# Graph attention in 13 parts from a ring of gathered rows

## The chip, the cores and the metric

The kernel runs on one core of a Trainium2 chip. The metric is the device time of one execution in microseconds (us). Engines are named as the profile names them: PE is the matrix engine, PEld its weight load, DVE the vector engine, ACT the scalar engine, POOL the GpSimd engine, SP the engine that here only issues transfers.

## The reference

The graph has 3125 nodes with 256 features each and 53125 edges, sorted by their destination. Four layers follow each other, each added to its input and normalized: a two-layer mean aggregation, three hops of weighted aggregation, an interaction layer with degree scaling, and graph attention with 8 heads of 32. The change is about the attention:

```python
src = jnp.concatenate([edge_index[0], loop])
dst = jnp.concatenate([edge_index[1], loop])
h = (x @ W).reshape(n, HEADS, OUT_DIM)
a_src = jnp.einsum('nhc,hc->nh', h, att_src)
a_dst = jnp.einsum('nhc,hc->nh', h, att_dst)
e = jax.nn.leaky_relu(a_src[src] + a_dst[dst], NEG_SLOPE)
m = jax.ops.segment_max(e, dst, num_segments=n)
e = jnp.exp(e - m[dst])
denom = jax.ops.segment_sum(e, dst, num_segments=n)
alpha = e / (denom[dst] + 1e-16)
out = jax.ops.segment_sum(h[src] * alpha[:, :, None], dst, num_segments=n)
```

Each node also has an edge to itself (the loop).

## The kernel before, in words

The edges are padded to 416 tiles of 128, the nodes to 25 tiles of 128. Each engine has its own instruction queue, written out in program order; engines wait for each other through semaphores.

The three hops (`hops_pe`, `hop_dve`, `hops_pool`) are six phases of matrix products on PE. DVE empties PSUM banks at the end of each phase (L1552) and applies the activation (L1585, L1590); between phases it prepares small tables for the attention and is otherwise idle. The layer after the hops ends with the projection `h` and the scores of each node; `write_heads` stores them tile by tile to the table `t_h`, whose row is 264 words: 8 heads of 32 values and one word that is 1.0 (`ATT_ROW`, `HEAD_ROW`).

The attention then goes through all edges twice.

1. The score stage. The score of each edge's source node is picked by one-hot products: in 112 steps DVE builds a one-hot of the low part of the index (L2298), PE multiplies the score table with it (L2226), DVE masks by the high part (L2311), and PE sums (L2237). The scores lie with 16 times 8 rows on the partitions and edges along the free dimension, so that a segment maximum is a forward and a backward scan (L2352, L2393, the latter over 3327 elements). Then come the joins between the 16 rows of edges (L2399 to L2409), the subtraction (L2412), transposes (L2415, L2419) and the exponentials on ACT (L2417). Meanwhile POOL gathers rows of `t_h` for part of the edge tiles with indirect DMAs, 128 rows each (L2134); since the final places are still in use as scratch, SP stores those rows to a DRAM table (`keep_rows`) and loads them back later (`load_rows`).

2. The merge. For each quad (4 edge tiles) DVE multiplies the gathered rows with their weights in place (`scale_rows`, L2486) and builds the one-hot of destination nodes (`node_hots`, L2492). Weights of even quads are read from SBUF (`hidden`), those of odd quads from PSUM (`banks`). PE adds each tile's product to a PSUM bank of its node tile (`merge_pe`, L2531): 440 steps, since a tile on a border between node tiles is multiplied twice. The places hold 16 quads; POOL gathers directly into those that are not staged. Early in the merge POOL also gathers the maximum of each node's last edge (`gather_last`, L2453, 25 times) and makes the exponents of the loops (`weigh_own`, L2458). ACT empties the node banks and adds the loop terms.

After the merge DVE divides, normalizes and adds, in seven groups of node tiles (`attended`, `inner_stats`, `inner_norm`, `store`).

## Time and profile before

| | us |
|---|---|
| median of 3 runs | 2983.28 (2981.79 to 2991.97) |
| span of the profiled execution | 2974.2 |
| hops, first to last eviction by DVE | 1122 to 1917 |
| first gather of the attention | 2186.5 |
| first scaling of the merge | 2564.0 |
| first instruction after the merge on DVE | 2900.1 |

The span is the time from the first to the last instruction of the one execution that was profiled; its own device time is not recorded beside it. The median of the runs is 9.1 us above the span, for what lies before the first instruction and behind the last. A busy time says how long an engine executed instructions; the idle time before an instruction is named with what ended it.

### The profile page before, as it was taken

To read this page: it belongs to the slowest core of one execution; us is meant where nothing else is said; L and a number is where in the kernel's file an instruction comes from. 1 tells how busy PE (TensorE), PEld (TensorE's weight loads), DVE (VectorE), ACT (ScalarE), POOL (GpSimd) and SP (SyncE) were. 2 spreads that over 40 slices of the span, in tenths; PEclk is the share of its full clock that TensorE was granted. 3 is DMA by queue.
4 is the path that set the end of the run, shared out by engine and by line. 5 is a ranking of instruction groups with operands and counts; after the bars stand their busy time and mean duration, and the time that the engine had idled before them with its cause. 6 is when DMAs were issued, how large, how long until landed. Compare 5 with 4: busy or idle time off the path is not lost. (4 is left out here: it accounts for less than half of the span.)

```text
span 2974.2 us, 32381 instructions
## 1 busy us (share of the span) xinstructions
PE 2470.6 (83%) x9483; PEld 1621.2 (55%) x9484; DVE 1396.0 (47%) x3940; ACT 707.2 (24%) x1552; POOL 936.7 (31%) x927
## 2 busy tenths in 40 slices
PE   3677789897987999999999999999977886457680
PEld 2444788343766555565556555577743444345560
DVE  7999656455665001030101001455575664546668
ACT  3776545111443000010001000255400000103112
POOL 0000256666666000000000000012167666576740
PEclk9888999998998999999999999999988998678885
DMA  6565678343344743444444434333558887646641
GB/s 233 243 253 225 212 238 264 118 138 97 112 121 137 152 151 129 151 134 151 129 152 133 151 119 145 93 106 102 113 168 271 278 282 245 209 132 190 192 127 43
DMA packets 209534, 493.89 MB, mean 166 GB/s; under 512 B 46457, under 2 KB 128430, under 8 KB 209134
## 3 DMA queue, kind: packets, MB, share of 16 engines
q1 hardware_dynamic: 135185, 301.30, 32.2%
q10 hardware_dynamic: 38173, 133.27, 12.8%
q0 software_dynamic: 36032, 57.60, 7.1%
q8 instruction: 67, 1.10, 0.1%
q14 instruction: 77, 0.63, 0.1%
HBM read 374.71 MB, written 117.32 MB: 165 GB/s over the span
## 5 line engine op out<-in xcount | busy, mean ns | idle before, releaser
L794 POOL DMA_INDIRECT table_dense_weights<-pair_weight,dst x416 | 411.2, 988 | 563.5 <-DVE weights_c L849 324.8
L1526 PE MATMUL banks<-own_term,features_and_rows 128*128 128x391 f32 (+1 forms) x1656 | 552.3, 491 | 0.0
L2134 POOL DMA_INDIRECT features_and_rows<-table_heads,src x376 | 401.7, 1068 | 191.4 <-issue 107.9
L1526 PEld LDWEIGHTS banks<-own_term,features_and_rows 128*128 128x128 f32 x1656 | 312.2, 189 | 226.8
L1552 DVE TENSOR_SCALAR features_and_rows<-banks,hop_bias 128x391 f32<-128x391 f32 (+1 forms) x24 | 15.0, 625 | 762.2 <-PE banks L1526 762.2
L954 PE MATMUL banks<-split_rows,count_columns 128*128 128x512 f32 x1200 | 322.1, 415 | 19.6 <-issue 12.6
L2531 PE MATMUL banks<-features_and_rows,edge_to_window 128*128 x880 | 233.4, 427 | 104.5 <-DVE edge_to_window L2492 71.6
L1526 PE MATMUL banks<-features_and_rows 128*128 128x391 f32 (+1 forms) x840 | 282.4, 491 | 0.0
L954 PEld LDWEIGHTS banks<-split_rows,count_columns 128*128 128x128 f32 x1200 | 226.3, 193 | 76.8 <-issue 21.7
L2531 PEld LDWEIGHTS banks<-features_and_rows,edge_to_window 128*128 128x128 f32 x880 | 181.3, 210 | 156.5 <-issue 122.5
L558 PE MATMUL banks<-features_and_rows,pair_and_bias_rows 128*128 128x400 f16 x806 | 184.3, 388 | 87.1 <-DVE features_and_rows L540 51.9
L936 ACT CAST count_columns<-hidden 128x640 fp32r<-128x640 f16 x310 | 212.4, 723 | 157.2 <-PE banks L954 62.2
L1526 PEld LDWEIGHTS banks<-features_and_rows 128*128 128x128 f32 x840 | 158.4, 189 | 114.6
L2004 POOL DMA_INDIRECT ble_values_at_first_edge<-dst,row_of_first_edge x50 | 48.0, 961 | 516.9 <-DVE ln_rstd L1983 464.9
L1601 POOL DMA_INDIRECT features_and_rows<-table_hop,node_of_tail_row x6 | 5.7, 953 | 638.1 <-DMA table_hop<-tmp 637.1
L558 PEld LDWEIGHTS banks<-features_and_rows,pair_and_bias_rows 128*128 128x128 f16 x806 | 110.8, 152 | 160.9 <-issue 147.6
L540 DVE TENSOR_SCALAR features_and_rows<-counter_fp,features_and_rows 128x400 f16<-128x400 f16 x806 | 198.4, 335 | 0.0
L2226 PE MATMUL banks<-features_and_rows,pair_weight 128*104 128x512 bf16 (+1 forms) x672 | 169.8, 393 | 29.9 <-DVE features_and_rows L2298 19.1
L1543 ACT ACTIVATE features_and_rows<-banks,hop_bias 128x391 f32<-128x391 f32 (+1 forms) x24 | 14.1, 587 | 728.1 <-PE banks L1526 728.1
L1080 PE MATMUL banks<-split_rows,count_columns 128*128 128x258 f32 (+1 forms) x1200 | 158.6, 291 | 13.4 <-issue 10.2
L2237 PE MATMUL banks<-edge_to_window,edge_weight 104*128 104x512 f32 (+1 forms) x224 | 123.1, 634 | 53.2 <-DVE edge_to_window L2311 32.1
L2226 PEld LDWEIGHTS banks<-features_and_rows,pair_weight 128*104 128x104 bf16 x672 | 89.8, 137 | 131.9 <-issue 75.4
(425 smaller groups left out, 3016.8 us busy)
## 6 DMA issues: line engine op xcount, KB each, us to landing
hidden<-table_counts SPq DMA_DIRECT2D x305, 160.0 KB
table_dense_weights<-weights_c ACTq DMA_DIRECT2D x26, 1600.0 KB, 5.7
own_term<-table_dense_weights SPq DMA_DIRECT2D x52, 782.0 KB
features_and_rows<-table_rows_by_edge SPq DMA_DIRECT2D x58, 528.0 KB
own_term<-table_dense_weights SPq DMA_DIRECT2D x34, 780.5 KB
pair_and_bias_rows<-table_edge_rows ACTq DMA_DIRECT2D x50, 512.0 KB
weights_c<-table_edge_rows ACTq DMA_DIRECT2D x50, 512.0 KB
table_rows_by_edge<-features_and_rows SPq DMA_DIRECT2D x48, 528.0 KB
```

The costliest lines, as they stand in the source:

```text
L540: made = e.tensor_scalar(hot_ring[:, s % HOTS, q, :], counter[:, 0:WIDE], steps_key[:, q, s:s + 1], None, ALU.is_equal)
L558: m = e.matmul(banks[:, bass.ds(bank_at, WIDE)], low_ring[:, s // LOWS_AT_ONCE % LOW_BLOCKS, :, 2 * (s % LOWS_AT_ONCE) + q], hot_ring[:, s ...
L794: e.indirect_dma_start(out=self.table, out_offset=bass.IndirectOffsetOnAxis(ap=self.place[:, t:t + 1], axis=0), in_=self.values[:, t:t + 1 ...
L936: e.copy(in_group(count_columns, g), in_group(slot_of(q), g)).then_inc(s_a_wide, 1)
L954: m = e.matmul(to[:, 0:2 * DIM], lhs_of(k), both_pieces(k), start=(k == first), stop=False, skip_group_check=True)
L1080: m = e.matmul(to(wide), count_columns[:, k, :], piece(k, h, wide), start=(k == 0 and h == 0), stop=False, skip_group_check=True)
L1526: m = e.matmul(psum[b][:, 0:wide], z_block(block)[:, f * P:(f + 1) * P], streamed[tile % STREAM][:, lo - from_column:lo - from_column + wi ...
L2004: e.indirect_dma_start(out=t_start[c], out_offset=bass.IndirectOffsetOnAxis(ap=start_at[:, j:j + 1], axis=0), in_=node_pair[:, j, c * HEAD ...
L2134: e.indirect_dma_start(out=to[:, k, :], out_offset=None, in_=t_h, in_offset=bass.IndirectOffsetOnAxis(ap=src[:, t:t + 1], axis=0)).then_in ...
L2226: m = e.matmul(psum[i % 2][head_rows, 0:n], table[:, q, c, :], low_hot[i % 2][c][:, 0:n], start=(c == 0 and q == 0), stop=(c == 1 and q == ...
L2237: e.matmul(psum[2 + b % 2][:, 0:n], sum_heads[head_rows, at:at + P], masked[i % 2][head_rows, 0:n], start=(r == 0), stop=(r == SCAN_ROWS - ...
L2531: e.matmul(banks[:, bass.ds(column_at, ATT_ROW)], onehot[:, k % UNROLL, :], wide_rows[:, bass.ds(row_at, ATT_ROW)], start=False, stop=Fals ...
```

## The change

The attention goes through the edges once, in 13 parts of 32 tiles (8 quads). `t_h` holds the source's score in the 33rd word of each head, so the gathered row itself brings it, and the 112 one-hot steps, the table of edge indices, and the DRAM table of staged rows go away. POOL gathers all 416 tiles in order into a ring of 80 tiles; a quad's place is free once the quad 20 before it has been merged. The condition is written as a count of merge steps: tiles of quad q may be gathered when 4q - 52 steps are done.

For each part, `weigh(b)` takes the scores out of the ring, turns them with PE (256 elements on the free dimension now), runs the scans, joins and exponentials, the exponential now as a polynomial on DVE, and writes weights to PSUM. `prepare(b + 1)` does what does not need the gathered rows of the next part; it stands between the fourth and the fifth quad of part b on DVE. All weights are read from PSUM. Each ring row has 8 words more, with which the merge also sums the exponents of the loops; `gather_last` and `weigh_own` are gone. Loop terms are added by POOL behind its last gather (`add_own`); its rows are loaded from `t_h` by SP after merge step 376 (node tiles 0 to 15) and 385 (the others).

Since a segment can cross a border between parts, the maximum at the 12 borders is found beforehand: for each border POOL gathers 128 rows of 3200 16-bit counts (819 KB) and DVE masks and reduces them (`near_fetch`, `near_counts`), six borders after the first hop's work and six after the second's, with 12 times 4 small operations of 800 elements and fewer at the end. POOL's gathers for the hops stand between them. The rows of destinations, 13 pieces of 1 KB per partition, are loaded in 16 transfers before the last two tiles of `write_heads`. The scatter of start values is one indirect DMA per node tile instead of two. Waits on a register's value are written with one more register operation. `keep_heads` has one copy of 8 elements more.

The core of the diff (indented less than in the file):

```diff
+RING_TILES = 80
+RING_AHEAD = 16
+RING_QUADS = RING_TILES // GROUP
+RING_ROW = ATT_ROW + HEADS
+PART_TILES = 32
+PARTS = EDGE_TILES // PART_TILES
...
+def near_fetch(b, known):
+    def pool(e):
+        if b == 0:
+            for ready in (*written, known):
+                e.wait_ge(*ready)
+        else:
+            e.wait_ge(*near_read[b - 1])
+        e.indirect_dma_start(out=near_rows.rearrange("p k n -> p (k n)"), out_offset=None, in_=t_count,
+                             in_offset=bass.IndirectOffsetOnAxis(ap=bound_at[:, b:b + 1], axis=0)).then_inc(s_near, 16)
+
+    pr.queue["pool"].append(pool)
+
+def near_counts(b, ready):
+    t = V(lambda e: e.tensor_scalar(near_hot, iota[:, :], bound_low[:, b:b + 1], None, ALU.is_equal), ready)
+    t = V(lambda e: e.tensor_tensor(near_rows, near_rows, near_hot.unsqueeze(1).broadcast_to([P, NODE_TILES, P]), ALU.mult),
+          (s_near, 16 * (b + 1)), t)
+    near_read[b] = V(lambda e: e.tensor_reduce(near_penalty[:, b, :], near_rows, AX_X, ALU.add), t)
+    return near_read[b]
...
+pr.queue["pool"].append(lambda e: hops_pool(e, 0))
+for b in range(BOUNDS // 2):
+    near_fetch(b, bound_known)
+    t = near_counts(b, t)
...
 merge_made = pr.op("dve", lambda e: e.scalar_tensor_tensor(
...
+pr.queue["pool"].append(lambda e: hops_pool(e, 1))
+for b in range(BOUNDS // 2, BOUNDS):
+    near_fetch(b, bound_known)
+    t = near_counts(b, t)
+pr.queue["pool"].append(lambda e: hops_pool(e, 2))
...
 def gather_rows(e):
     e.wait_ge(*w_h)
...
+    for quad in range(QUADS):
+        if quad >= RING_QUADS:
+            e.wait_ge(*merged((quad - RING_QUADS) * GROUP + GROUP - 1))
+        for t in range(quad * GROUP, (quad + 1) * GROUP):
+            e.indirect_dma_start(out=ring_rows[:, ring_at(t), 0:ATT_ROW], out_offset=None, in_=t_h,
...
-    weigh_own(e)
-    gather_direct(e, [q for q in DIRECT_QUADS if q >= PLACES])
-
-def keep_rows(e, some):
-    for n in some:
...
+def add_own(e):
+    for n, g in enumerate(node_groups):
+        rows_of, weights_of = own_rows(g)[:, :, :, 0:HEAD_DIM], tiles(p_self, g)
+        e.wait_ge(s_own_back[g[0] // 16], 16)
+        e.wait_ge(s_summed, g[-1] + 1)
+        e.tensor_tensor(rows_of, rows_of, weights_of.unsqueeze(3).broadcast_to([P, len(g), HEADS, HEAD_DIM]), ALU.mult
+                        ).then_inc(s_own_scaled, 1)
+        e.wait_ge(s_own_scaled, n + 1)
+        sums_of = sum_rows(g)[:, :, :, 0:HEAD_DIM]
+        e.tensor_tensor(sums_of, sums_of, rows_of, ALU.add).then_inc(s_owned, 1)
...
+def prepare(b):
+    before = pr.last("dve")
+    seg_made = V(lambda e: e.tensor_tensor(seg[:, 1:], by_dst[:, b, 0:LAST], by_dst[:, b, 1:], ALU.subtract), scaled_dst, before)
+    for c in range(2):
+        held_read[b] = V(lambda e, c=c: e.tensor_tensor_scan(held_in[:, c, :], seg, psum[4][:, c * SCAN_LEN:(c + 1) * SCAN_LEN],
+                                                             first_value[:, b, c:c + 1], ALU.add, ALU.max),
+                         held_turned[b], (s_first_value, 32), seg_made)
+    V(lambda e: e.tensor_scalar(begins_here, start_values[b % 2][:, :, :, 0], -0.1 * BIG, None, ALU.is_gt), (s_start[b % 2], 16 * (b // 2 + 1)))
+    V(lambda e: e.tensor_scalar(flags[:, 0, :], by_dst[:, b, :], by_dst[:, b, 0:1], -1.0, ALU.subtract, ALU.mult), scaled_dst)
+    V(lambda e: e.tensor_scalar(flags[:, 1, :], by_dst[:, b, :], by_dst[:, b, LAST:], None, ALU.subtract))
+    for w in range(2):
+        V(lambda e, w=w: e.tensor_scalar(end_mask[:, w, 2 * P:], bound_key, end_key[:, b, w:w + 1], -BIG, ALU.not_equal, ALU.mult))
+        masked_ends[b] = V(lambda e, w=w: e.tensor_scalar(end_mask[:, w, 0:2 * P], keys_of, end_key[:, b, w:w + 1], -BIG,
+                                                          ALU.not_equal, ALU.mult), keys_spread[b])
+    for j in range(2 * b, min(2 * b + 2, NODE_TILES)):
+        V(lambda e, j=j: e.tensor_tensor(x[:, j, :], x[:, j, :], brow[:, B_BETA, :], ALU.add))
+
...
+def turn_scores(b):
+    landed = [row_landed(quad) for quad in part_quads(b)]
+    for lo, hi, at in pieces_of(b):
+        t = V(lambda e, lo=lo, hi=hi, at=at: e.tensor_copy(
+            in_rows(packed, lo, hi), by_row(ring_rows[:, at:at + hi - lo, HEAD_DIM:ATT_ROW:HEAD_ROW])), *landed)
+    for i in range(SCAN_TILES):
+        m = T(lambda e, i=i: e.transpose(a_turned[:, i * P:(i + 1) * P], packed[:, i, :], ident[:, :]), t, masked_ends[b])
+    return m
...
+def weigh(b):
+    m = turn_scores(b)
+    t = V(lambda e: e.tensor_tensor(met, a_turned, held_in[:, 1, :], ALU.add), m, held_read[b])
+    t = V(lambda e: e.scalar_tensor_tensor(out=bent, in0=met, scalar=0.2, in1=met, op0=ALU.mult, op1=ALU.max), t)
+    t = V(lambda e: e.tensor_tensor(met, bent, held_in[:, 0, :], ALU.max), t)
+    scanned = V(lambda e: e.tensor_tensor_scan(prefix, seg, met, -BIG, ALU.add, ALU.max), t)
+    V(lambda e: e.tensor_copy(back[:, LAST:], prefix[:, LAST:]), scanned)
+    spread_max = V(lambda e: e.tensor_tensor_scan(back[:, 0:LAST][:, ::-1], seg[:, 1:][:, ::-1], prefix[:, 0:LAST][:, ::-1],
+                                                  prefix[:, LAST:], ALU.add, ALU.max), scanned)
+    for w, at in enumerate((0, LAST)):
+        m = T(lambda e, w=w, at=at: e.matmul(end_values[:, w * P:(w + 1) * P], back[:, at:at + 1].broadcast_to([P, P]), ident[:, :],
+                                             start=True, stop=True), spread_max)
+    t = V(lambda e: e.tensor_tensor(at_ends, end_mask, all_values.unsqueeze(1).broadcast_to([P, 2, ALL_KEYS]), ALU.add),
+          m, masked_ends[b], bound_spread)
+    t = V(lambda e: e.tensor_reduce(end_value[:, :], at_ends, AX_X, ALU.max), t)
+    for w in range(2):
+        t = V(lambda e, w=w: e.scalar_tensor_tensor(out=back, in0=flags[:, w, :], scalar=end_value[:, w:w + 1], in1=back,
+                                                    op0=ALU.add, op1=ALU.max), t)
+    of_tiles = lambda to, i: to.rearrange("p (r i) h -> p i r h", i=SCAN_TILES)[:, i, :, :]
+    for i in range(SCAN_TILES):
+        max_turned = T(lambda e, i=i: e.transpose(of_tiles(max_of, i), back[:, i * P:(i + 1) * P], ident[:, :]), t)
+    gap = met
+    t = V(lambda e: e.tensor_tensor(gap, bent, back, ALU.subtract), t)
+    t = V(lambda e: e.tensor_scalar(power, gap, LOG2_E, -126.0, ALU.mult, ALU.max), t)
+    t = V(lambda e: e.tensor_scalar(rounded, power, ROUNDER, None, ALU.add), t)
+    scaled = V(lambda e: e.tensor_scalar(scale_i.bitcast(I32), rounded, ROUNDER - 127.0, float(1 << 23), ALU.subtract, ALU.mult), t)
+    t = V(lambda e: e.scalar_tensor_tensor(out=rest_of, in0=rounded, scalar=ROUNDER, in1=power, op0=ALU.subtract, op1=ALU.subtract), t)
+    t = V(lambda e: e.tensor_scalar(power, rest_of, EXP2[-1], None, ALU.mult), t)
+    for k in range(len(EXP2) - 2, 0, -1):
+        t = V(lambda e, k=k: e.scalar_tensor_tensor(out=power, in0=power, scalar=EXP2[k], in1=rest_of, op0=ALU.add, op1=ALU.mult), t)
+    t = V(lambda e: e.scalar_tensor_tensor(out=gap, in0=power, scalar=EXP2[0], in1=scale_i, op0=ALU.add, op1=ALU.mult), t, scaled)
+    for i in range(SCAN_TILES):
+        m = T(lambda e, i=i: e.transpose(of_tiles(weight_of, i), gap[:, i * P:(i + 1) * P], ident[:, :]), t)
+    own_gap = by_tile(rounded)
+    begins = start_values[b % 2][:, :, :, 0]
+    max_read[b] = t = V(lambda e: e.tensor_tensor(by_row(own_gap), in_rows(begins, 0, PART_TILES), by_row(max_of), ALU.subtract), max_turned, scaled)
+    for lo, hi, at in pieces_of(b):
+        cuts_read[b] = V(lambda e, lo=lo, hi=hi, at=at: e.tensor_tensor(
+            by_row(ring_rows[:, at:at + hi - lo, ATT_ROW:RING_ROW]), in_rows(begins_here, lo, hi), by_row(own_gap[:, lo:hi, :]),
+            ALU.mult), t)
+    for lo, hi, at in pieces_of(b):
+        V(lambda e, lo=lo, hi=hi, at=at: e.tensor_copy(ring_rows[:, at:at + hi - lo, HEAD_DIM:ATT_ROW:HEAD_ROW],
+                                                       weight_of[:, lo:hi, :]), m)
+
...
+def scale_rows(e, quad):
+    rows_of = quad_rows(quad)[:, :, :, 0:HEAD_DIM]
+    lo = quad * GROUP % PART_TILES
+    e.tensor_tensor(rows_of, rows_of, weight_of[:, lo:lo + GROUP, :].unsqueeze(3).broadcast_to([P, GROUP, HEADS, HEAD_DIM]), ALU.mult)
+
+def node_hots(e, quad):
+    lo = quad % 2 * GROUP
+    if quad >= 2:
         e.wait_ge(s_mm, quad * GROUP + (mm0 - GROUP))
     e.tensor_tensor(onehot[:, lo:lo + GROUP, :], counted_up.unsqueeze(1).broadcast_to([P, GROUP, P]),
-                    step_dst[:, bass.ds(quad * GROUP, GROUP)].unsqueeze(2).broadcast_to([P, GROUP, P]),
+                    step_dst[:, quad * GROUP:(quad + 1) * GROUP].unsqueeze(2).broadcast_to([P, GROUP, P]),
                     ALU.is_equal).then_inc(s_hot, 1)
...
+turn_start(0)
+prepare(0)
+for b in range(PARTS):
+    weigh(b)
+    if b + 1 < PARTS:
+        turn_start(b + 1)
+    if b == 0:
+        pr.queue["dve"].append(lambda e: e.wait_ge(*count_kept))
+    if b + 1 < PARTS:
+        pr.queue["dve"].append(lambda e, b=b: merge_dve(e, step_quads(b)[0:GROUP]))
+        prepare(b + 1)
+        pr.queue["dve"].append(lambda e, b=b: merge_dve(e, step_quads(b)[GROUP:]))
+    else:
+        pr.queue["dve"].append(lambda e, b=b: merge_dve(e, step_quads(b)))
+    pr.queue["pe"].append(lambda e, b=b: merge_pe(e, b))
 pr.queue["act"].append(merge_act)
-pr.queue["dve"].append(merge_dve)
```

## Rows read from the trace of the kernel before

**Rows 1.** the first line of the page: the whole profiled execution.

```profile
span 2974.2 us, 32381 instructions
```

**Rows 2.** stretches of the attention: us, busy us (instructions) by engine, granted clock, DMA.

```profile
2186.00:2564.00 378.00, 281.03 (x1008) 150.96 (x1008) 227.82 (x445) 8.85 (x16) 256.52 (x247) 0.85 0.78 252
2564.00:2626.00 62.00, 25.84 (x76) 18.37 (x76) 17.81 (x19) 3.06 (x9) 42.31 (x44) 0.72 0.50 171
2626.00:2900.00 274.00, 205.26 (x796) 161.01 (x797) 175.22 (x195) 54.39 (x227) 171.08 (x156) 0.88 0.56 174
```

**Rows 3.** POOL in the attention by line: busy us, mean ns, idle before.

```profile
L2134 POOL DMA_INDIRECT features_and_rows<-table_heads,src x376 | 401.7, 1068 | 191.4 <-issue 107.9 <-DVE edge_to_window L2311 31.8 <-PE banks L2531 28.9
...
L2453 POOL DMA_INDIRECT tmp<-table_running_max,row_of_last_edge x25 | 24.6, 984 | 7.6 <-issue 7.6
```

**Rows 4.** timeline of POOL: start us, us, instruction, idle before.

```profile
2186.54 0.98 POOL L2134 DMA_INDIRECT features_and_rows<-table_heads,src  x1 [0.30 <-issue]
...
2584.39 0.95 POOL L2134 DMA_INDIRECT features_and_rows<-table_heads,src  x1 [0.30 <-issue]
...
2623.91 0.60 POOL L2458 TENSOR_TENSOR tmp<-dst,tmp 128x200 f32<-128x200 f32 x1 [1.36 <-DMA tmp<-table_running_max,row_of_last_edge]
```

**Rows 5.** timeline of DVE and POOL, a gather beside a scaling.

```profile
2835.20 1.25 DVE L2486 TENSOR_TENSOR features_and_rows<-features_and_rows,hidden 128x1056 f32<-128x1056 f32 x1
...
2835.44 1.83 POOL L2134 DMA_INDIRECT features_and_rows<-table_heads,src  x1 [0.30 <-issue]
...
2840.55 1.24 DVE L2486 TENSOR_TENSOR features_and_rows<-features_and_rows,banks 128x1056 f32<-128x1056 f32 x1
...
2841.14 0.95 POOL L2134 DMA_INDIRECT features_and_rows<-table_heads,src  x1 [0.30 <-issue]
```

**Rows 6.** timeline of POOL, first and last of nine gathers beside a DVE chain.

```profile
2547.09 1.09 POOL L2134 DMA_INDIRECT features_and_rows<-table_heads,src  x1 [0.30 <-issue]
...
2559.43 1.28 POOL L2134 DMA_INDIRECT features_and_rows<-table_heads,src  x1 [0.30 <-issue]
```

**Rows 7.** DVE in the merge and just before, by line and shape.

```profile
L2492 DVE TENSOR_TENSOR edge_to_window<-banks,dst_of_step 128x512 f32<-128x512 f32 x110 | 75.9, 690 | 142.4 <-remote 64.6 <-PE banks L2531 48.3 <-issue 29.3
...
L2486 DVE TENSOR_TENSOR features_and_rows<-features_and_rows,banks 128x1056 f32<-128x1056 f32 x52 | 64.7, 1244 | 0.0
...
L2412 DVE TENSOR_TENSOR own_term<-own_term,features_and_rows 128x512 f32<-128x512 f32 x6 | 4.1, 692 | 0.2
...
L2404 DVE TENSOR_REDUCE key_of_row_end<-weights_c 128x1 f32<-128x256 f32 x2 | 0.8, 420 | 0.1
```

**Rows 8.** timeline of DVE and PE at the end of the score stage.

```profile
2535.07 0.42 DVE L2350 TENSOR_TENSOR tmp<-own_term,weights_c 128x256 f32<-128x256 f32 x1
...
2535.53 0.75 DVE L2352 TENSOR_TENSOR_SCAN features_and_rows<-features_and_rows,tmp 128x256 f32<-128x256 f32 x1
...
2543.58 0.79 PE L2397 MATMUL banks<-identity,features_and_rows 128*128 128x128 f32 x2 [9.47 <-DVE features_and_rows L2393]
...
2544.84 0.76 DVE L2402 TENSOR_TENSOR weights_c<-banks,weights_c 128x256 f32<-128x256 f32 x2 [1.31 <-PE banks L2399]
```

**Rows 9.** the chain that ended last, a run of merge products.

```profile
2656.70 9.11 PE banks L2531 x38
```

**Rows 10.** timeline of PE, the first products after an idle time.

```profile
2629.46 3.88 PE L2531 MATMUL banks<-features_and_rows,edge_to_window 128*128 x8 [14.32 <-issue]
```

**Rows 11.** timeline of DVE in the hops: first eviction of two phases.

```profile
1440.59 0.63 DVE L1552 TENSOR_SCALAR features_and_rows<-banks,hop_bias 128x391 f32<-128x391 f32 x1 [141.77 <-PE banks L1526]
...
1759.76 0.62 DVE L1552 TENSOR_SCALAR features_and_rows<-banks,hop_bias 128x391 f32<-128x391 f32 x1 [160.91 <-PE banks L1526]
```

**Rows 12.** DMA issues by line: KB each, median us to landing.

```profile
table_counts<-hidden SPq DMA_DIRECT2D x25, 800.0 KB, 3.3
```

**Rows 13.** DVE in the first stage, a 16-bit operation.

```profile
L537 DVE TENSOR_TENSOR pair_and_bias_rows<-features_and_rows 128x1024 f16<-128x1024 f16 x99 | 69.4, 701 | 9.0 <-PE banks L558 8.7
```

**Rows 14.** timeline of DVE, the first instruction after the merge.

```profile
2900.07 1.25 DVE L2576 TENSOR_TENSOR own_term<-own_term,hidden 128x1056 f32<-128x1056 f32 x1
```

882 lines of the change are left out of this document (306 added, 576 removed).

## Prediction

> **What bounds the kernel now.** I read the page first, then the stretches, then POOL and DVE by line, and last the timelines of both engines beside each other. The span is 2974.2 us [rows 1]. The attention lies between 2186 and 2900 us, and no engine fills it: in the score stage (378 us) PE is busy for 281 and DVE for 228, then come 62 us in which DVE is busy for 18, then 274 us of merge with PE at 205 and POOL at 171 [rows 2]. The reader should see a stage limited by the ping-pong of DVE and PE, a gap, and a merge that waits for rows. Behind it is POOL: it makes 416 gathers of about 1.07 us each (376 in the row that stands here) and then 25 more for the maxima, and sits idle between them, mostly because its places are not free [rows 3]. Undisturbed, a gather takes 0.95 us and the next follows 0.30 later, so one per 1.25 us [rows 4]: all 416 would need 520 us against the 714 that the attention takes.
>
> **What slows a gather.** One gather beside a scaling with both operands in SBUF (L2486 with `hidden`) takes 1.83 us and ends 0.82 after that scaling; one beside a scaling with its weights in PSUM (`banks`) takes 0.95 [rows 5]. Nine gathers beside the chain of L2409 and L2412, SBUF operands only, start 12.34 us apart in 8 steps: 1.54 each, 0.29 more than undisturbed [rows 6].
>
> **The change, part by part.**
>
> *POOL's period.* 32 gathers at 1.25 are 40.0 us. The merge takes its weights from PSUM now and doesn't hold them up. In `weigh` and `prepare` some 25 operations without a PSUM operand remain, about 10.4 us of a part. Of 32 gathers about 8 fall there, and the 256-wide operations are shorter than those of rows 6, so I charge 0.2 each: 1.8. The period is 41.8 us. Bounds: 40.0 (no hindrance), and 40 + 10.4 = 50.4 if no gather gets through in that time.
>
> *DVE and PE in a period.* A quad costs DVE 1.78 (three quads from 2835.20 to 2840.55 [rows 5]); 1024 elements scaled instead of 1056 make it 1.75. PE needs 9.11 / 19 = 0.48 us a step [rows 9], with 272 columns for 264 0.495, a quad 1.98. After an idle time it needs 3.88 / 4 = 0.97 a step [rows 10], so 1.0, for 4 to 5 steps. Counted from the end of `weigh`: quad 0 is ready at 1.75 and done at 5.75; quad 1 ends at 8.25 (one slow step); quad 2 at 10.2, quad 3 at 12.2; the one-hots are double-buffered, so quad 3's wait for quad 1 until 8.25 and end at 8.9. `prepare` then takes 5.2: a subtraction and two additions at 0.46, two scans at 0.78 [rows 8], two PSUM masks at 0.46, five single-input operations at 0.2 to 0.3. Quad 4 is ready at 15.85, PE has been idle for 3.7 and is slow again: quads 4 to 7 end at 19.85, 22.4, 24.3, 26.3.
>
> `weigh`: 16 operations of 256 elements start 0.46 apart (2535.07 to 2535.53), 7.4 us; two scans at 0.78, 1.6; a copy of one column 0.1; one addition of 704 elements by the 512-wide row, 704/512 x 0.69 = 0.95, one reduction of 704 by 704/256 x 0.42 = 1.15 [rows 7, 8]. Four single-input operations have no row of their width here: between nothing and 0.46, I take 0.3, 1.2 in all. Three times DVE waits for PE, 1.31 each [rows 8]; the third wait has 0.9 of work beside it: 3.0. Sum 15.4. The first transposes stand on PE behind the merge of the part before, so from the last step on 14.9 are left. The period of this loop is 26.3 + 14.9 = 41.2 us.
>
> The two loops agree within 0.6 us, and the ring lets POOL run ahead: the next part's last quad may be gathered when the third quad of this one is merged, 10 us after `weigh`. I take 42.0 us.
>
> *The sum.* Start of gathers 2186.5 [rows 4]; the later loads of destinations (16 transfers on SP ahead of the last two tiles) and one copy more per tile: 1.0 (0 to 8). First part: 34 gathers at 1.25 and 1 us of hindrance, 43.5; the first `prepare` is done beside it. 12 x 42.0 = 504.0. The last gather's landing: 1.4 after its end [rows 4]. `weigh(12)` 15.4. The last merge has 14 quads and no `prepare`; DVE is free when the last one-hots are built, behind quad 11: 8.25 + 10 x 1.98 + 0.65 = 28.7. The end of the kernel took 2974.2 - 2900.1 = 74.1 [rows 1, 14]; two additions of 1.25 with their gaps go: 71.5.
>
> *Loops' terms on POOL.* 14 operations stand behind the last gather. POOL's row is 0.60 us for 200 elements [rows 4]; 1024 elements are at most five times that, 3.1. Eight of them can begin when 2.1 MB have landed, in the middle of `weigh(12)`. Whether they hold up DVE's SBUF operations no row shows: 0 to 24 us. The merge isn't affected, its operands include PSUM. I take 8.
>
> 2186.5 + 1.0 + 43.5 + 504.0 + 1.4 + 15.4 + 28.7 + 71.5 + 8 = 2860.0 us of span. With 9.1 between span and median: **2869 us**, 3.8% less than 2983.3.
>
> *The borders of parts* are costed at nothing, because DVE is idle for 141.8 us before one hop eviction and for 160.9 before the other [rows 11]. One border: the gather 1.25, landing 3.3 for the same volume in the nearest row [rows 12], a mask 0.2, 3200 16-bit elements 3200/1024 x 0.70 = 2.2 [rows 13], their reduction 3200/256 x 0.42 = 5.25 [rows 7]: 12.2. Six are 73; the second six with 27 us of small operations are 100. The cover is gone from 22 us a border on. POOL's hop gathers wait behind these, but for block 24 of a phase only. What the register operation costs in the first stage isn't seen here; PE waits there for DVE in part, and I take nothing.
>
> **A rule against this change.** The rows show that DVE's SBUF operations hold back gathers; in the other direction L2412 kept its 0.69 beside gathers [rows 6, 7]. The Trainium skill (SBUF — State Buffer, section "SBUF: two separate sides") says that DVE and GpSimd share a pair of ports as an exclusive lock: whichever starts first has it for the whole instruction, and the other blocks fully. By the trace's gathers the period is 41.8; by this rule in its strict reading it would be the period of rival D.
>
> **The rivals.**
>
> A. *PE stays at its lower clock.* Granted clock is 0.72 where PE has gaps and 0.88 in the merge [rows 2]. If every step took 1.0 us, a quad takes 4.0: 5.75 + 28 + 14.9 = 48.7 a part, 6.7 x 12 = 80, and 22 in the last merge: 2971. For it: `weigh` leaves PE idle for 13 us. Against: rows 9 stand within a merge with gaps, and steps are fast there. Half of it, 2895 to 2940, is likelier than the whole.
>
> B. *The borders come late* and DVE holds up the hops. At twice my price (24.4 a border) 5 and 12 us are missing: 2886. Slower reductions can do that.
>
> C. *POOL gets no gather through beside `weigh` and `prepare`*: 50.4 a part, 12 x 8.4 = 101 more: 2970. Against: rows 6.
>
> D. *Gathers hold up DVE.* Each of the 25 SBUF operations of a part waits for the gather in hand, 0.48 on average (half of 0.95): 41.2 + 12 = 53.2 a part, 12 x 11.2 = 134: 3003, slower than before. It decides from 0.40 us an operation on, a period of 51.5. Against: 0.69 of L2412 beside gathers.
>
> E. *The ring doesn't run ahead*, gather, `weigh` and merge follow one another: 40 + 1.4 + 15.4 + 26.3 = 83 a part, 12 x 41 = 492: 3361. Against: the condition 4q - 52 leaves 52 tiles open.
>
> F. *Less than my sum*: period 40, no cost for the loops' terms: 2837.
>
> **How the numbers follow.** The forecast, 2845 to 2895: 0.63. Partly A 0.16, wholly A 0.04, B 0.04, C 0.03, D 0.04, E 0.02, F 0.04. The range 2845 to 2935 holds the forecast, most of A's middle and B: 0.8. Half a per cent, 15 us, is about what a measurement of this kernel can tell from no change. Faster (below 2968): 0.63 + 0.16 + 0.04 + 0.04 = 0.87; A whole and C are at its edge: 0.07 same; D and E 0.06 slower.
>
> **What would show it.** In the changed kernel's trace: first gather within 8 us of 2186.5; gathers mostly 0.95 in the merge quads and longer in `weigh`; starts of `weigh` 40 to 44 us apart; the last gather near 2735; PE slow only for the first steps after each idle time; hop evictions where they were; DVE's first instruction after the merge near 2788. The prediction is wrong if `weigh` takes over 20 us (small operations or PE's answers cost more), if evictions shift, or if POOL waits for merge steps.

## The result: 1.8% slower where it was first measured, 1.3% faster on another chip

| | kernel before | changed | ratio, 95% interval |
|---|---|---|---|
| first chip | 2987.16 us (2981.79 to 2991.97) | **3043.61 us** (3034.55 to 3056.63) | **1.018** (1.014 to 1.022) |
| another chip, the same two kernels | 2803.41 us | **2766.53 us** (2764.44 to 2768.77) | **0.987** (0.985 to 0.989) |

Predicted were 2869 us and a ratio of 0.962. The result on record is the first line, and the prediction is wrong. The second line came with the experiments. The kernel before itself took 2987 us on the first chip, 2993 and 2979 (one run each) on two chips of later runs (one of them may be the first), and 2799 to 2804 on four others. The 6.6% between the two kinds are the key to this case, and the trace of before held a sign of it. Whether they belong to the chip itself or to its state at that time no run tells: only one chip was met twice, both times with about 2800.

First the changed kernel on the first chip: the first line of its profile, then stretches (us, busy us and instructions of PE, PEld, DVE, ACT and POOL, granted clock, DMA share and GB/s): POOL's first gather to the first `weigh`, the twelve periods, `weigh(12)` with the last merge, the tail:

```profile
span 3037.8 us, 30296 instructions
```

```profile
2198.10:2246.00 47.90, 2.90 (x11) 2.31 (x11) 13.94 (x20) 0.00 (x0) 37.23 (x36) 0.50 0.37 92
2246.00:2904.60 658.60, 318.51 (x972) 222.01 (x973) 355.51 (x641) 16.82 (x62) 371.27 (x383) 0.65 0.31 84
2904.60:2965.40 60.80, 34.20 (x136) 25.85 (x134) 46.51 (x51) 2.06 (x9) 24.89 (x12) 0.78 0.18 56
2965.40:3037.80 72.40, 0.02 (x1) 0.00 (x0) 63.07 (x208) 18.82 (x42) 2.66 (x3) 0.52 0.13 44
```

A period is the time from one `weigh` to the next, one part of the edges. Twelve periods take 658.6 us, 54.9 each on average, where the forecast had 42.0; that is 155 of the 175 us of the miss. Nine of them take 52.9 to 53.5 us; the first takes about 85, the fifth 59 and the last 39. No engine is full in them. The lines of the part loop, with the idle time before them and what ended it (compare [rows 3, 7]):

```profile
L2345 DVE TENSOR_TENSOR edge_to_window<-banks,dst_of_step 128x512 f32<-128x512 f32 x110 | 75.5, 687 | 208.4 <-remote 126.5 <-PE banks L2372 43.9 <-issue 37.8
L2149 POOL DMA_INDIRECT row_ring<-table_heads,src x416 | 406.5, 977 | 310.0 <-PE banks L2372 144.6 <-issue 111.2 <-remote 34.8
L2372 PE MATMUL banks<-row_ring,edge_to_window 128*128 x880 | 293.7, 495 | 212.3 <-DVE edge_to_window L2345 116.7 <-issue 89.2 <-ACT banks L2387 6.1
```

DVE, POOL and PE each wait for another. The gathers themselves are as priced (0.98 us, nearly unhindered), and so are the elementwise operations. But DVE's one-hots wait 164 us for something that the profile calls "remote" (a semaphore was raised just then, but no instruction of the profile ends near it) or "issue" (it shows nothing that was waited for). One part's second half in the timeline (start, us, idle before):

```profile
2684.54 4.83 PE L2372 MATMUL banks<-row_ring,edge_to_window 128*128 x13
...
2688.61 0.69 DVE L2345 TENSOR_TENSOR edge_to_window<-banks,dst_of_step 128x512 f32<-128x512 f32 x1 [2.32 <-PE banks L2372]
...
2689.62 1.99 PE L2372 MATMUL banks<-row_ring,edge_to_window 128*128 x6 [0.25 <-issue]
...
2693.03 0.72 PE L2372 MATMUL banks<-row_ring,edge_to_window 128*128 x2 [1.41 <-issue]
...
2699.21 0.96 POOL L2149 DMA_INDIRECT row_ring<-table_heads,src  x1 [0.30 <-issue]
2701.99 0.69 DVE L2345 TENSOR_TENSOR edge_to_window<-banks,dst_of_step 128x512 f32<-128x512 f32 x1 [11.57 <-remote]
2702.23 0.95 POOL L2149 DMA_INDIRECT row_ring<-table_heads,src  x1 [2.06 <-remote]
...
2703.01 3.98 PE L2372 MATMUL banks<-row_ring,edge_to_window 128*128 x8 [9.27 <-DVE edge_to_window L2345]
...
2709.09 0.18 ACT L2383 ACTIVATE weights_c<-banks 128x8 f32<-128x8 f32 x1 [31.13 <-remote]
...
2709.37 0.95 POOL L2149 DMA_INDIRECT row_ring<-table_heads,src  x1 [2.40 <-remote]
2709.37 0.42 DVE L2294 TENSOR_TENSOR weights_c<-banks,weights_c 128x256 f32<-128x256 f32 x1 [6.41 <-remote]
```

Every one-hot uses a buffer that two quads before had: at 2701.99 DVE waits for products of the row that ends at 2689.4. The record of the semaphore that these products raise explains it. Its updates, in us:

```
first chip:  2688.58 2690.72 2693.55 2697.77 2701.97 2704.80 2707.63 2709.07 .11 .16 .20 .24 .28
other chip:  2424.40 2424.86 2425.32 2425.78 2426.24 2426.70 2427.15 2427.61 2428.07
```

A normal step is 0.46 us behind the last. Here they come 1.4 to 5.6 us apart, in multiples of about 0.70, and 113 of PE's register instructions have records of about 0.70 us in this trace (one has in the other chip's). I call these **slow steps**. Some 60 updates of the 440 steps of the merge are missing in this record (none on the other chip), so one of these distances can hold more than one step; that the updates come late is shown by the engines that wait for them. The ends of the matmul rows are modelled and show only gaps marked "issue". Three engines start within 0.3 us of 2709.1, because the updates left over arrive in a burst. In ten of the twelve parts such a burst ends a stretch of slow steps, in nine of them 2 to 4 us after POOL's last gather before a pause (in the first part 11 us): POOL pauses from 2707.0 to 2709.4, from 2647.3 to 2651.1 (burst 2650.8), from 2380.5 to 2384.6 (burst 2384.4). The stretch begins some 11 to 13 us after POOL has begun to issue without a pause. One distance of 4.0 to 4.5 us stands in every part on the other chip too: there PE waits for DVE's `prepare`, and it is not a slow step.

The same kernel on the other chip, the same lines:

```profile
2144.60:2638.70 494.10, 282.99 (x984) 214.67 (x984) 357.42 (x641) 17.54 (x63) 372.62 (x383) 0.73 0.42 116
```

```profile
L2345 DVE TENSOR_TENSOR edge_to_window<-banks,dst_of_step 128x512 f32<-128x512 f32 x110 | 75.5, 686 | 42.9 <-PE banks L2372 42.3
L2149 POOL DMA_INDIRECT row_ring<-table_heads,src x416 | 407.7, 980 | 141.6 <-issue 116.4 <-DMA table_heads<-features_and_rows 15.1 <-PE banks L2372 10.1
L2372 PE MATMUL banks<-row_ring,edge_to_window 128*128 x880 | 253.5, 455 | 56.9 <-DVE edge_to_window L2345 56.4 <-issue 0.5
```

No "remote", no "issue" on DVE's one-hots. A period is 41.2 us, POOL's 32 gathers at 1.26 and a little. POOL never waits for the ring: none of the idle times before its gathers that end with PE is over 0.30 us, what lies between any two gathers.

### The profile page after: what moved, and what is told of

The parts are those of the page before. It is cut to its first block, busy times and chain, and to the rows that moved or that the text cites. A ratio compares the mean times of both kernels' runs of the same rounds, so it can differ in the third digit from the quotient of the medians.

```text
span 3037.8 us, 30296 instructions
## 1 busy us (share of the span) xinstructions
PE 2304.3 (76%) x8708; PEld 1531.0 (50%) x8708; DVE 1474.7 (49%) x4063; ACT 661.3 (22%) x1371; POOL 895.4 (29%) x901
## 4 chain that ended last, share of the span: by engine, by line
PE 59%; DVE 23%; another core or an unknown queue 8%; issue 6%; DMA 1%; ACT 1%; POOL 1%; SPq 1%; ACTq 0%; DVEq 0%
PE banks L1517 27%; PE banks L2372 6%; DVE features_and_rows L555 6%; PE banks L939 5%; PE banks L1065 5%; PE banks L1182 2%; PE banks L1197 2%; DVE features_and_rows L1245 2%; PE banks L1504 2%; PE banks L1487 2%; DVE pair_and_bias_rows L552 2%; PE banks L1957 1%; DVE row_ring L2339 1%; DVE ln_stats L744 1%
## 5 line engine op out<-in xcount | busy, mean ns | idle before, releaser
L2149 POOL DMA_INDIRECT row_ring<-table_heads,src x416 | 406.5, 977 | 310.0 <-PE banks L2372 144.6
L2372 PE MATMUL banks<-row_ring,edge_to_window 128*128 x880 | 293.7, 495 | 212.3 <-DVE edge_to_window L2345 116.7
L2372 PEld LDWEIGHTS banks<-row_ring,edge_to_window 128*128 128x128 f32 x880 | 202.7, 241 | 298.5 <-issue 251.4
L939 PEld LDWEIGHTS banks<-split_rows,count_columns 128*128 128x128 f32 x1200 | 224.5, 192 | 78.1 <-issue 17.2
L1619 POOL DMA_INDIRECT hidden<-table_counts,edge_weight x12 | 11.4, 946 | 637.4 <-DVE edge_weight L1628 341.1
L2345 DVE TENSOR_TENSOR edge_to_window<-banks,dst_of_step 128x512 f32<-128x512 f32 x110 | 75.5, 687 | 208.4 <-remote 126.5
L2049 POOL DMA_INDIRECT ble_values_at_first_edge<-dst,row_of_first_edge x25 | 24.4, 977 | 506.2 <-DVE ln_rstd L2028 487.7
L1065 PEld LDWEIGHTS banks<-split_rows,count_columns 128*128 128x128 f32 x1200 | 149.2, 193 | 20.9 <-issue 19.5
```

The lines of the kernel that those rows point to most:

```text
L939: m = e.matmul(to[:, 0:2 * DIM], lhs_of(k), both_pieces(k), start=(k == first), stop=False, skip_group_check=True)
L1065: m = e.matmul(to(wide), count_columns[:, k, :], piece(k, h, wide), start=(k == 0 and h == 0), stop=False, skip_group_check=True)
L2149: e.indirect_dma_start(out=ring_rows[:, ring_at(t), 0:ATT_ROW], out_offset=None, in_=t_h, in_offset=bass.IndirectOffsetOnAxis(ap=src[:, t: ...
L2345: e.tensor_tensor(onehot[:, lo:lo + GROUP, :], counted_up.unsqueeze(1).broadcast_to([P, GROUP, P]), step_dst[:, quad * GROUP:(quad + 1) * ...
L2372: e.matmul(banks[:, bass.ds(column_at, RING_ROW)], onehot[:, s % UNROLL, :], ring[:, bass.ds(row_at, RING_ROW)], start=False, stop=False, ...
```

## The experiments

**1. Four variants, on a chip that turned out to have no slow steps** (before: 2799; one run of each). Without the later gathers, and without the waits for their landing:

```
-            for quad in range(QUADS):
-                if quad >= RING_QUADS:
-                    e.wait_ge(*merged((quad - RING_QUADS) * GROUP + GROUP - 1))
+            for quad in range(RING_QUADS):
```

> Leaves out every gather after the first 20 quads: the merge of the later quads reads whatever lies in the ring, all else is as in the changed kernel. In the changed kernel a part takes 53 us, and in its second half single merge steps finish 1.4 to 5.6 us apart (multiples of 0.70 us) while POOL issues gathers without a pause; each such stretch ends with a burst of updates 2 to 4 us after POOL pauses. Theory G (gathers on their way hold up PE's sequencer and its semaphore updates): without gathers the slow steps are gone from the third part on, a part takes weigh 14 + prepare 4.2 + eight quads of 1.9 + about 2 of handing over = 35 to 41 us, and the kernel ends 110 to 180 us earlier, at 2860 to 2930. Theory F (PE's merge written out as straight code has to be fetched, and the fetch is late): the slow steps stay, a part stays over 50 us, and the time above 3010. Theory C (the granted clock, 0.5 in half of the stretch): the period stays within 3 us of 53.

Measured 2721 us, parts of 35.5 to 37.6, mostly 37.5. No theory of the slow steps is tested, since there were none. But it measures the loop of DVE and PE by itself: 37.5 us, where I had 41.2. A repeat on a chip with 2804 gave 2722.

Later gathers with a quarter of the bytes:

```
+                    full = quad < RING_QUADS
+                    ... out=ring_rows[:, ring_at(t), 0:ATT_ROW if full else ATT_ROW // 4]
+                    ... in_=t_h if full else t_h[:, :].rearrange("n (q c) -> (n q) c", q=4)
```

> Gathers of the first 20 quads are whole rows of 264 values; every later gather takes 66 values a row (from a quarter of the table), so the values merged are others. Number of gathers, rows and waits is that of the changed kernel. It tells the two halves of theory G apart. If the bytes of the gathers do it, the slow steps of 1.4 to 5.6 us go from the third part on and the period falls from 53 to 35 to 43 us (POOL's own loop is 32 x 1.26 = 40.3), time 2870 to 2940. If it is the issuing or the number of rows, the slow steps and the 53 us stay, time 3010 to 3050. Theory F (code fetch) and theory C (clock) expect 53 us too.

2762 us, a part 40.9: POOL's time for a gather (0.97 us on average) doesn't depend on its bytes.

PE's code as a loop:

```
-            for s in steps: ...
+            with e.Fori(0, many // UNROLL) as i:
+                e.load(pe_regs[0:UNROLL], merge_control[0:1, bass.ds(i * UNROLL + first, UNROLL)])
+                for k in range(UNROLL): ...
```

> PE's merge of each part as a loop of 8 steps with one load of 8 registers, in place of 32 steps of straight code with loads of 16; the same steps, waits and result. Theory F (fetch of straight code): slow steps gone, a part 38 to 42 us, time 2880 to 2920. Theory G (gathers on their way) and theory C (clock): slow steps stay at 1.4 to 5.6 us, a part 53 to 57 us (two more loads of registers of about 0.7 us and four branches a part), time 3030 to 3090.

2768 us, parts of 41.1, which looked like theory F. The control below takes that away: the straight code on a like chip takes 2767.

PE's steps at fixed places (the loads and the wait before each step go, the evictions move behind the last step):

```
-                e.matmul(banks[:, bass.ds(column_at, RING_ROW)], onehot[:, s % UNROLL, :], ring[:, bass.ds(row_at, RING_ROW)],
+                e.matmul(psum[0][:, 1:1 + RING_ROW], onehot[:, s % UNROLL, :], ring[:, at:at + RING_ROW],
```

> PE's merge steps take fixed places: no register loads, no register arithmetic, no wait for a begun bank; all steps add into one bank, and ScalarE evicts the banks only after the last step, so the sums are others and some 20 us of evictions come behind the last step. PE's sequencer then has a matmul of two passes a step where it had three register instructions and a wait before it. Theory G with a price for each instruction or event of PE (0.70 us each; 6 to 8 of them a step in the changed kernel): slow steps of at most 2.8 us, a part 42 to 47 us. Theory G with a price for each step: slow steps of 4 to 5.6 us stay, a part 50 to 54. Theory C: a part 50 to 54. Theory F: less code a part (by more than half), so fewer slow steps, 42 to 48.

2777 us, parts of 41.1: POOL's loop again.

**2. The control: the changed kernel on such a chip.**

> The changed kernel itself, once more. The four kernels before this one ran on a chip on which the kernel before takes 2799 us and not 2987, and none of them shows the slow merge steps, the one with nothing changed but PE's code in a loop neither. Theory G' (the slow steps come with gathers on some chips only, in both kernels): on a chip where the kernel before takes about 2799, the changed one has no slow steps, a part takes 41 us (POOL's loop), and the time is 2765 to 2790, ratio 0.985 to 0.997; on a chip where the kernel before takes about 2987, it is 3035 to 3055 again. Theory F (fetch of the straight code, on any chip): slow steps and 53 us a part here too, time 2900 or more.

2766.53 us, ratio 0.987. The straight code alone doesn't bring slow steps, as theory F (code fetch) has it; the chip, or its state, makes the difference.

**3. The kernel before on such a chip.**

> The kernel before, for its trace on this chip; only the four kinds of waits on a loaded value are written with a masked register, as the changed kernel has them, one register instruction each. Theory G': where its time is near 2800, no merge step is over 1.5 us late for no reason that the trace shows, its merge (339 us long in the first trace) takes 60 to 80 us less, and the earlier stages with gathers beside PE (first 1010 us) some 100 us less; near 2987 both are as in the first trace. If the masks themselves cost something (about 440 + 300 register instructions), its time is over that of the kernel before by more than 0.5%.

2798 us (the chip's runs of before as it stands: 2804, 2799 to 2809), so the masks cost nothing that shows. Its stretches stand here below those of the first chip: the stage in which POOL makes 416 other gathers beside PE, the hops without gathers, the scores and the merge, both with gathers.

```profile
323.00:978.00 655.00, 563.87 (x2600) 411.54 (x2601) 372.48 (x1219) 233.13 (x424) 410.98 (x416) 0.93 0.51 158
989.00:1917.00 928.00, 925.15 (x2922) 546.13 (x2921) 85.05 (x245) 50.22 (x115) 5.72 (x6) 1.00 0.45 139
2187.00:2564.00 377.00, 281.03 (x1008) 150.96 (x1008) 226.86 (x441) 8.85 (x16) 255.82 (x246) 0.85 0.78 253
2564.00:2903.00 339.00, 234.09 (x884) 181.59 (x884) 195.86 (x220) 57.44 (x236) 213.39 (x199) 0.85 0.55 172
```

```profile
324.00:902.00 578.00, 546.36 (x2670) 404.99 (x2669) 370.62 (x1222) 235.56 (x426) 410.03 (x416) 0.98 0.58 182
892.00:1819.00 927.00, 924.45 (x2922) 545.99 (x2920) 84.76 (x244) 49.64 (x114) 11.96 (x13) 1.00 0.45 139
2088.00:2425.00 337.00, 261.20 (x1012) 146.15 (x1012) 228.38 (x443) 11.15 (x21) 257.64 (x242) 0.87 0.87 291
2425.00:2725.00 300.00, 213.51 (x880) 162.50 (x880) 194.08 (x220) 55.15 (x229) 218.23 (x203) 0.93 0.59 185
```

With gathers 77, 40 and 39 us apart; without them 1 us in 928. (The windows are cut by hand; at the first eviction of the hops the two are 97 us apart, at 1122.4 and 1025.1.) The bursts of updates mark the same stages: in the first trace of before 40 updates of the merge come less than 0.1 us behind the last, here none; in the changed kernel 45 on the first chip and none on the other. And the idle time of the one-hots in the merge, 142.4 us in [rows 7], 94 of it "remote" or "issue":

```profile
L2496 DVE TENSOR_TENSOR edge_to_window<-banks,dst_of_step 128x512 f32<-128x512 f32 x110 | 75.3, 684 | 14.9 <-PE banks L2535 14.8
```

**4. The same variants on chips with slow steps.** Without the later gathers:

> No gathers after the first 20 quads, for a chip on which the kernel before takes about 2987 us (its first two runs were on chips with 2799 and 2804, and took 2721 and 2722). There, Theory G' expects the slow merge steps only until the first 80 gathers are issued, then parts of 36 to 39 us, and 2850 to 2910 in all, against 3043 of the changed kernel. If the slow steps belong to that chip whatever POOL does, parts of 50 us and over 2990. On a chip with 2800 again: 2721.

2876 us beside 2993 of before. The period falls from 80.8 us (the first part, beside its gathers) to 35.5 to 37.5, and no step is slow any more:

```profile
2254.60:2335.40 80.80, 24.92 (x71) 17.07 (x72) 29.38 (x53) 0.84 (x3) 44.84 (x47) 0.58 0.31 84
2335.40:2742.00 406.60, 252.40 (x904) 194.68 (x903) 324.56 (x590) 16.27 (x59) 0.00 (x0) 0.75 0.03 7
```

The first part still ends with a burst, 12 us after the last gather; from the second part on the only distances between 1.2 and 7 us are those of `prepare`, 3.9 to 4.2 us, one a part. So it takes gathers, on such a chip, to make steps slow. A low clock alone (theory C) would not do: after an idle time a step takes about 1.0 us [rows 10], a slow one up to 5.6. The next three ran on the chip with 2979.

> On the chip with slow merge steps (before 2993): gathers after the first 20 quads take 66 values a row and not 264; their number, their rows and their waits stay. The bytes do it: slow steps gone from the third part on, a part 41 us (POOL's loop, as this kernel has on the other chips), 2900 to 2940 in all. The issuing and the number of rows do it: a part stays at 51 to 54 us, 3030 to 3050. On a chip with 2800: 2762.

3029 us, parts of 52 to 53 behind the first: not the bytes. The DMA moved 25 GB/s in these parts where the changed kernel moved 84, and DVE waited as before (from 2290 us on):

```profile
L2347 DVE TENSOR_TENSOR edge_to_window<-banks,dst_of_step 128x512 f32<-128x512 f32 x108 | 74.1, 686 | 218.2 <-remote 127.8 <-PE banks L2374 47.0 <-issue 43.2
```

> On the chip with slow merge steps: PE's merge steps at fixed places, no register loads, no register arithmetic, no waits for banks; evictions behind the last step. Slow steps of the changed kernel are 1.4 to 5.6 us in multiples of 0.70. If each instruction of PE's sequencer pays 0.70 us, a step of one matmul in two passes with its weights pays at most 2.8 us and a part takes 42 to 48 us, 2930 to 3000 in all with the later evictions; if each step pays, the parts stay at 50 to 54 us, 3030 to 3070. On a chip with 2800: 2777.

3092 us, parts of 53 to 65, longer than with the register instructions; distances of up to 6.3 us between updates, where a price of 0.70 for each instruction allowed 2.8. The price is not one for each instruction of PE; why the parts are longer isn't settled.

One wait for a bank a quad:

```
-                e.wait_ge(s_begun, step & 31)
+                    e.wait_ge(s_begun, last & 31)        # once, where s % GROUP == 0
```

> On the chip with slow merge steps: the changed kernel with one wait for a begun bank, and one register instruction for it, a quad in place of four of each; all else and the result are the same. A price of 0.70 us an instruction: slow steps of 4.2 and 5.6 us become 2.8 and 4.2 us, a part takes 46 to 50 us, 2960 to 3010 in all. A price a step: 53 us and 3035 to 3050. On a chip with 2800, where POOL sets the period: 2762 to 2768.

3035 us, parts of 53: the same answer. This trace has 16 register instructions with records of about 0.70 us, where the changed kernel has 113, for the same period: those records go with the slow steps and are not what they cost.

**5. The terms that were off on every chip.** SyncE's order:

```
-                if n == NODE_TILES - 1:
-                    ... load_scan_dst(e, row)        # 16 of them
                 write_heads(e, n)
+            ... load_scan_dst(e, row)                # behind the loop
```

> SyncE issues the last two tiles' rows and node values before the 16 loads of the edges' destinations and not after them. In the changed kernel the 16 issues take 11 us, POOL's first gather waits 15.1 us for the row tables and starts at 2096.8. Theory Q (the queue order costs what my term of 1.0 us left out): the first gather starts 10 to 15 us earlier and the whole ends 9 to 15 us earlier, on a chip where POOL's loop sets the period (ratio to the kernel before 0.982 to 0.984 where the changed one has 0.987). Rival: the tables' landing itself takes these 15 us, or the first part's preparation, whose loads now come later, is late: within 3 us of the changed kernel.

2752.65 us, ratio 0.982 (0.980 to 0.984), 14 us less than the changed kernel, and 15 less than its variant with `prepare` moved (below), which ran on this very chip. POOL's first gather starts 18 us earlier. The changed kernel on a like chip, then this one:

```profile
2096.84 2.38 POOL L2149 DMA_INDIRECT row_ring<-table_heads,src  x1 [15.09 <-DMA table_heads<-features_and_rows]
```

```profile
2078.86 0.99 POOL L2148 DMA_INDIRECT row_ring<-table_heads,src  x1 [0.30 <-DMA table_heads<-features_and_rows]
```

DVE now waits for the destinations until 2114.80, and the first `weigh` starts 52.8 us behind the first gather, not 47.8; but the first period is 36.5 and not 41 us, and in the two traces the last step comes 17.7 us earlier.

The landing records split the 18 us. The last tile's rows are issued at 2082.72 and land at 2096.57, 13.85 us later; with heads first they are issued at 2076.86 and land at 2078.57, 1.71 us later. So 6 us are the issues in the queue, and 12 are the landing behind 16 transfers of 104 KB. The rival of this run had the landing take all of the time whatever the order; the landing is the larger share, but only with the loads ahead of it.

POOL's adds on one column of each head:

> POOL's nine scalings and additions of the nodes' own rows take one column of each head's 32 and not all, so the sums lack most of the own rows; the loads and waits are those of the changed kernel. Theory H (POOL's elementwise work holds up DVE's operations in SBUF during the last weighing): the last weighing takes 14 us as the others and not about 30, and the end comes 13 to 20 us earlier. Rival (hidden: the last evictions and the tail set the end anyway): within 4 us of the changed kernel.

2750 us (one run), 16 less than the changed kernel and 17 less than the next run on the same chip; `weigh(12)` takes 14.0 us, not 24.4.

> The next part's preparation stands before the part's quads and not in their middle. Where POOL's loop sets the period (a part 41 us; DVE and PE alone 37.5), nothing changes: within 3 us of the changed kernel, ratio 0.986 to 0.989 where that has 0.987. If the middle place itself bought time (PE finishes a backlog of steps beside it), a part takes 1 to 4 us longer and the whole 12 to 40 us. On a chip with slow merge steps POOL waits for the merge, and 4 us more or less a part would show: 10 to 50 us later.

2767.43 us, ratio 0.987 (0.985 to 0.988): where the next part is prepared makes no difference where POOL sets the period.

**6. A better version**, the new order of SyncE and the adds behind the last weighing:

```
+        def add_own(e):
+            e.wait_ge(*weighed_last[0])              # DVE's last operation of weigh(12)
             ...
```

> On top of the heads-first order: POOL begins to scale and add the nodes' own rows only when DVE's last weighing is done, so that they fall beside the last merge, 56 steps that bound PE for 28 us while DVE needs 20. With the adds beside it the last weighing took 30 us and with one column each 14. Theory H (POOL's elementwise work holds up DVE where they meet, and DVE has 8 us to spare in the last merge): the last weighing takes 14 us again, the last merge 28 to 34, the whole 8 to 16 us less than heads-first alone, ratio 0.976 to 0.979 where that has 0.982. Rival: the same sum of hold-ups is paid in the last merge or in the tail, which waits for the added groups: within 3 us of heads-first, or up to 5 us more.

**2740.07 us, ratio 0.9785** (0.977 to 0.980), the fastest of the kernels that do all the work. `weigh(12)` takes 14 us again, and the last merge 31.8, 0.8 longer than with heads first alone. On a chip with slow steps:

> The heads-first order with the own rows added beside the last merge, for a chip on which the kernel before takes about 2987 us. The two edits take 28 us off on a chip with 2800. Theory G' leaves them as they are there (neither has to do with gathers beside PE's steps): 3043 less 20 to 30 = 3013 to 3023, still slower than before. If instead the parts shrink as well, to under 48 us, under 2987. On a chip with 2800 again: 2738 to 2742.

3009 us beside 2993, one run each: 34 less than 3043, which was on the first chip, and still no gain there; a part takes 54 on average.

**7. A pause for POOL**, meant for a chip with slow steps; this one (2801) has none, so both tell only a price.

> POOL waits after every second quad until its rows have landed: a pause of 1.5 to 2.5 us in every 10. On a chip with slow merge steps (2980 to 2993 before) they set in some 12 us after POOL begins to issue without a pause, and end with a burst 2.3 to 3.7 us after it pauses. If a pause as such clears them, they never set in: a part takes POOL's 40.3 + 4 x 2 = 48 us, and the whole 2970 to 2990. If the pauses are too short to clear them: 53 us or more, 3040 to 3090. On a chip without slow steps (2800 before), where POOL sets the period: 46 to 50 us a part, 2830 to 2885, the price of the pauses.

2860 us, some 48 a part; a pause is 2.1 us, within the 1.5 to 2.5 expected.

> One tiny operation of POOL (a memset of one value a row) behind every gather, so that gathers come every 1.5 to 1.7 us and not every 1.26. If the rate of the gathers brings the slow steps on, a chip that has them shows none or few: a part takes POOL's 48 to 53 us with PE's and DVE's work hidden below it, 2960 to 3030 in all. If any gathering beside PE brings them on, they stay and come on top: 56 us or more, over 3070. On a chip without slow steps: 48 to 53 us a part, 2850 to 2920.

2763 us, a part 41, where 48 to 53 were expected: the memset (0.12 us) fits into the 0.30 us that POOL leaves between two gathers, and paced nothing. Neither run met slow steps, so whether pauses or a slower pace of gathers would avoid them is not tested.

## Why the prediction was wrong, step by step

| term of the sum | predicted | first chip | other chip |
|---|---|---|---|
| start of gathers | 2187.5 | 2198.1 | 2096.8 |
| first part and landing | 44.9 | 47.9 | 47.8 |
| twelve periods | 504.0 | **658.6** | 494.1 |
| `weigh(12)` and the loops' terms | 23.4 | 29.3 | 24.4 |
| last merge | 28.7 | 31.5 | 31.1 |
| tail | 71.5 | 72.4 | 72.4 |
| span to median | 9.1 | 5.8 | -0.1 |
| sum | 2869 | 3043.6 | 2766.5 |

**The step that failed: "PE needs 9.11 / 19 = 0.48 us a step", and 1.0 for four or five steps after idle time.** That holds only on chips without slow steps. On the first chip updates come 1.4 to 5.6 us apart for the second half of a part, and 13.7 us of each part go on average (54.9 against 41.2). The range ended at 2935, and no rival had this mechanism. The prediction had the signs in its rows: 14.32 us of PE's idle time "issue" [rows 10], and 94 of the one-hots' 142 us "remote" and "issue" [rows 7]. I took the duration from those rows (3.88, 690 ns) and left their last column. It said that in the kernel before, too, DVE waited for products that PE had been given long before.

**Why it costs the change more.** From the first gather of the attention to the end:

| | slow steps | none | |
|---|---|---|---|
| kernel before (without slow steps: with masks) | 787.7 | 708.2 | 79.5 us apart |
| changed | 839.7 | 669.8 | 169.9 us apart |
| changed less before | +52.0 | -38.4 | |

What lies ahead of it loses about 100 us in either kernel (98.4 and 101.3), so the sign of the result is decided in the attention. In the kernel before, half of the scalings hold gathers back [rows 5]; here none does, and POOL issues for some 25 to 30 us of each part without a pause. That this is why the change loses more was argued from the traces, not tried by itself.

**The model without it.** With before's start of gathers on a chip without slow steps (2088.1) in place of 2186.5, the same sum gives a span of 2762; measured were 2766.6. Part of that agreement is luck: the start is 8 us later than in the sum and the first part 3 longer, while the twelve periods are 10 shorter. The prediction's 3.8% was then wrong a second way: it was held against a kernel before that was slowed by 184 us, on the assumption that its first 2186 us and none of its waits would matter. Span against span (2762 and 2801.6) it is about 1.4%, and 1.3% came. The term of 9.1 between span and median was misread too: in the runs that have both, the time is only 1.8 to 2.2 us above the span, so the other 7 us say that the profiled execution of before was faster than the median, not what lies outside the span.

**Start of gathers, 1.0 (0 to 8): missed.** The hops came 6.1 us earlier, but SyncE issues the 16 loads in 11.76 us, ahead of the last two tiles' rows:

```profile
2165.79 11.76 SPq L1913 DMA_DIRECT2D own_term<-dst_run  x16
2177.59 2.00 SPq L1925 DMA_DIRECT2D table_heads<-features_and_rows  x1
...
2180.58 0.97 SPq L1925 DMA_DIRECT2D table_heads<-features_and_rows  x1
```

The first gather starts at 2198.1, 18 us after the 2180.4 that the earlier hops would have allowed. By experiment 5 a third of such a delay is the queue and two thirds are the slower landing of the last rows behind the 16 transfers. I had named the queue, had not multiplied 16 by the time of an issue, and had left out that the transfers themselves stand ahead.

**The loops' terms, 8 (0 to 24): the right size** (10.4 of `weigh(12)` by experiment 5, 16 of the whole), and a mechanism that no row had shown. First DVE with the adds on one column, then DVE and POOL of the changed kernel on the first chip:

```profile
2642.75 0.42 DVE L2313 TENSOR_TENSOR weights_c<-weights_c 128x256 f32<-128x256 f32 x1
2643.20 0.29 DVE L2314 TENSOR_SCALAR tmp<-weights_c 128x256 f32<-128x256 f32 x1
```

```profile
2917.08 2.02 DVE L2314 TENSOR_TENSOR weights_c<-weights_c 128x256 f32<-128x256 f32 x1
2919.13 2.34 DVE L2315 TENSOR_SCALAR tmp<-weights_c 128x256 f32<-128x256 f32 x1
2921.51 1.88 DVE L2316 TENSOR_SCALAR tmp<-tmp 128x256 f32<-128x256 f32 x1
2923.43 2.41 DVE L2317 TENSOR_SCALAR tmp<-tmp 128x256 int32<-128x256 f32 x1
```

```profile
2918.90 2.42 POOL L2168 TENSOR_TENSOR hidden<-hidden,row_ring 128x1024 f32<-128x1024 f32 x1
2921.29 1.95 POOL L2164 TENSOR_TENSOR row_ring<-row_ring,weights_c 128x1024 f32<-128x1024 f32 x1
```

Operations of 0.29 and 0.42 us take as long as POOL's beside them. The Trainium skill (SBUF — State Buffer, section "SBUF: two separate sides") calls the ports that the two share an exclusive lock for a whole instruction; it names for it DVE's two-port modes and its operations with two SBUF inputs, a condition that the prediction left out. For POOL's elementwise work the trace agrees.

Its gathers don't hold up DVE: a `weigh` takes 14.0 us beside gathers on either kind of chip, and so does the last one of the better version, with neither gathers nor adds beside it. In experiment 4 without gathers, from its first addition to the last step of the polynomial it takes 11.0 to 11.5 us, the same as with them. Rival D was wrong, though its 3003 was the nearest number and its period of 53.2 is, by luck, what most periods measured. (The 51.5 at which it "decides" should be 51.2.)

**The rest.** `weigh` 14.0 (15.4 predicted), DVE and PE's loop 37.5 (41.2), POOL's 40.9 (41.8), tail 72.4 (71.5). The borders of parts were hidden: the evictions of the hops come 6 us earlier than before, and DVE's idle time before the two in question falls to 78 and 73 us. The granted clock (rival A) was 0.73 in the periods of the other chip, where no time was lost. The ring did run ahead (against E); POOL waited for merge steps, as my list of signs had it, but because the steps were slow.

## What to carry to other kernels

Read the last column: idle time that ends with "remote" or "issue" behind an engine that has long been given its work is a cost of its own, and a price per step taken from the rows between such gaps leaves it out. Before a ratio is predicted, the model must also give the time of the kernel before; undisturbed prices would probably have led to about the 2800 of the other chips and not to 2987, but I didn't work it out. For a moved load, multiply the number of transfers by an issue's time, add the time in which their bytes move, and ask what stands behind them.
